# Low attention products of 64 columns between the transposes, and a later head's projection between the two halves

## What is computed

```
xn     = group_norm(x, 32 groups) * w + b
q,k,v  = W_qkv @ xn + b_qkv           # 8 heads of 64 channels
weight = softmax(q^T k * scale)       # 1024 x 1024 for each head
a      = weight @ v
x      = x + W_proj @ a + b_proj
```

## Time and profile before

| | us |
|---|---|
| median of 3 runs | 4347.31 (4347.17 to 4347.99) |
| span of the profiled execution | 4346.0 |
| PE busy in it | 4295.6 |
| DVE / ACT / POOL busy | 3313.6 / 2875.3 / 2505.1 |
| time of the chain that ended last that is PE's | 95% |

### The profile page before, as it was taken

The page is one execution under the profiler, slowest core; times in us unless marked ns, Lnnn a source line. Parts: engine busy times, 40 slices in busy tenths (PEclk is TensorE's granted clock), DMA queues, the critical chain, the costliest instruction groups (busy, mean ns, idle before and its releaser), DMA issues.

```text
span 4346.0 us, 89905 instructions
## 1 busy us (share of the span) xinstructions
PE 4295.6 (99%) x26692; PEld 3736.9 (86%) x26692; DVE 3313.6 (76%) x5483; ACT 2875.3 (66%) x5317; POOL 2505.1 (58%) x2406
## 2 busy tenths in 40 slices
PE   7999999999999999999999999999999999999999
PEld 6888888888888888888888888888888888888887
DVE  5777867788687786777867778687786877868778
ACT  4757747477474775747757476574765747667476
POOL 5655556565564655656566565565655646556465
PEclk9999999999999999999999999999999999999999
DMA  3232222322223222222222222222222222223222
GB/s 87 48 96 47 71 72 48 96 47 80 64 46 96 49 78 64 56 86 49 80 71 66 81 46 80 65 66 79 48 79 64 71 71 49 79 64 82 60 49 92
DMA packets 99933, 295.61 MB, mean 68 GB/s; under 512 B 15136, under 2 KB 15264, under 8 KB 99616
## 3 DMA queue, kind: packets, MB, share of 16 engines
q1 hardware_dynamic: 99616, 291.71, 25.0%
HBM read 123.88 MB, written 33.55 MB: 36 GB/s over the span
## 4 chain that ended last, share of the span: by engine, by line
PE 95%; DVE 2%; issue 1%; POOL 1%; ACT 1%; DMA 0%; SPq 0%; DVEq 0%; ACTq 0%; POOLq 0%
PE ps_t L760 21%; PE ps_g L714 15%; PE ps_o L772 11%; PE ps_o L773 11%; PE ps_s L751 11%; PE ps_s L749 11%; PE ps_s L714 7%; PE ps_t L714 6%; PE ps_o L714 3%; POOL x_raw L389 1%; ACT probs L479 0%; DVE spread L603 0%; DVE pt_lo L569 0%; DVE work L601 0%; PE ps_t L778 0%
## 5 line engine op out<-in xcount | busy, mean ns | idle before, releaser
L383 POOL TENSOR_SCALAR probs<-probs,row_rcp 128x1024 f32<-128x1024 f32 x1024 | 1149.9, 1123 | 1375.5 <-DVE row_rcp L564 1374.0
L560 DVE TENSOR_REDUCE row_min<-ps_s 128x1 f32<-128x1024 f32 x1024 | 1250.2, 1221 | 220.5 <-PE ps_s L751 205.0
L484 ACT CAST pt_hi<-ps_t 128x512 fp32r<-128x512 f32 x2048 | 1110.6, 590 | 446.5 <-PE ps_t L760 431.7
L569 DVE TENSOR_TENSOR pt_lo<-ps_t,pt_hi 128x512 fp32r<-128x512 f32 x2048 | 1308.5, 679 | 9.5 <-ACT pt_hi L484 5.0
L479 ACT ACTIVATE probs<-ps_s,row_min 128x1024 f32<-128x1024 f32 x1024 | 1150.7, 1124 | 215.5 <-DVE row_min L560 202.5
L760 PEld LDWEIGHTS ps_t<-const_sb,probs 128*128 128x128 f32 x8192 | 944.3, 140 | 185.5 <-DVE pt_lo L569 57.0
L760 PE MATMUL ps_t<-const_sb,probs 128*128 128x128 f32 x8192 | 1085.9, 274 | 0.8
L772 PE MATMUL ps_o<-pt_hi,v_st 128*128 128x256 f32 x4096 | 1044.4, 288 | 0.0
L773 PE MATMUL ps_o<-pt_lo,v_st 128*128 128x256 f32 x4096 | 1014.8, 282 | 0.0
L751 PE MATMUL ps_s<-kl_st,q_st 128*128 128x512 f32 x2048 | 808.3, 395 | 0.0
L772 PEld LDWEIGHTS ps_o<-pt_hi,v_st 128*128 128x128 f32 x4096 | 771.6, 188 | 39.4 <-issue 12.4
(11 more groups left out here) (110 smaller groups left out, 4918.2 us busy)
## 6 DMA issues: line engine op xcount, KB each, us to landing
wqk_raw<-in_wqk SPq DMA_DIRECT2D x130, 256.0 KB, 2.7
q_st<-kh_st SPq DMA_DIRECT2D x128, 256.0 KB, 2.9
q_st<-kl_st SPq DMA_DIRECT2D x128, 256.0 KB, 3.6
kh_st<-kh_st SPq DMA_DIRECT2D x128, 256.0 KB, 2.9
kl_st<-kl_st SPq DMA_DIRECT2D x128, 256.0 KB, 3.5
x_raw<-layer_out SPq DMA_DIRECT2D x36, 512.0 KB, 5.0
wv_raw<-in_wv SPq DMA_DIRECT2D x68, 256.0 KB, 3.6
x_raw<-in_x SPq DMA_DIRECT2D x32, 512.0 KB, 5.3
```

Of the source, the lines that this page charges most:

```text
L383: nc.gpsimd.tensor_scalar(probs[m % 2][:, :], probs[m % 2][:, :], row_rcp[:, m % 4:m % 4 + 1], 1.0, ALU.mult, ALU.mult).then_inc(probs_rea ...
L484: nc.scalar.copy(pt_hi[:, m // 2 % 2, 4 * half:4 * half + 4, (m % 2) * P:(m % 2 + 1) * P], ps_t[:, half, :].rearrange("p (b t) -> p b t", ...
L560: nc.vector.tensor_reduce(row_min[:, m % 4:m % 4 + 1], ps_s[:, m % 2, :], AX.X, ALU.min).then_inc(min_ready, 1)
L569: nc.vector.tensor_tensor(pt_lo[place], ps_t[:, half, :].rearrange("p (b t) -> p b t", b=4), f32(pt_hi[place]), ALU.subtract).then_inc(lo_ ...
```

## The change

- `weigh` is split up. The low product of a block (`weigh_low`) takes only the 64 columns of v's high part as the stationary operand and writes partitions 0 to 63 of `ps_o`; the product of v's low part and the probabilities' low part is left out. In odd steps each transpose has one low product behind it. The high products of the group stand in the even step before (seven) and at the end of the odd step (one). Group 7 has its products in the order high, eight low, seven high.
- `later_qk` (and in the last pair the output projection's parts of steps 0 and 1) stands between the transposes of the first and those of the second half, in all steps, where it stood behind both.
- The bias of v moves from `evac_v`, which becomes a copy, to `add_halves`, which becomes one instruction with a scalar operand. `bv_all` and its broadcast transfer of 512 KB give way to `bv_sb`, with 4 KB.

```diff
-            def transpose(n, m):
-                pe.wait_ge(probs_ready, n + 1)
-                for half in range(2):
-                    pe.wait_ge(lo_ready, lo_at(n - 1, half))
-                    for b in range(4):
-                        mm = nc.tensor.transpose(...)
-                    mm.then_inc(transposed, 1)
-            def weigh(tile, g, hd, k, lo, hi):
-                if lo == 0:
-                    pe.wait_ge(attn_ready, sum_at(g - 1))
-                    pe.wait_ge(v_ready, hd + 1)
-                    pe.wait_ge(lo_ready, lo_at(tile + 2 * k + 1, 1))
-                for b in range(lo, hi):
-                    v = v_st[k // 4][:, b, :]
-                    nc.tensor.matmul(ps_o[:, 0:GROUP], v, pt_hi[:, k % 2, b, :], start=(b == 0), stop=False)
-                    mm = nc.tensor.matmul(ps_o[:, 0:GROUP], v, pt_lo[:, k % 2, b, :], start=False, stop=(b == BLK - 1))
+            def transpose(m, c):
+                mm = nc.tensor.transpose(ps_t[:, c // 4, (c % 4) * P:(c % 4 + 1) * P],
+                                         probs[m % 2][:, c * P:(c + 1) * P], ident)
+                if c % 4 == 3:
+                    mm.then_inc(transposed, 1)
+            def weigh_high(k, b):
+                mm = nc.tensor.matmul(ps_o[:, 0:GROUP], v_st[k // 4][:, b, :], pt_hi[:, k % 2, b, :],
+                                      start=(b == 0), stop=(b == BLK - 1))
+                if b == BLK - 1:
+                    mm.then_inc(pv_done, 1)
+            def weigh_low(k, b):
+                nc.tensor.matmul(ps_o[0:D, 0:GROUP], v_st[k // 4][:, b, 0:D], pt_lo[:, k % 2, b, :],
+                                 start=False, stop=False)
+            def group_free(tile, g, hd, k):
+                pe.wait_ge(attn_ready, sum_at(g - 1))
+                pe.wait_ge(v_ready, hd + 1)
+                pe.wait_ge(lo_ready, lo_at(tile + 2 * k + 1, 1))
+            def transpose_and_weigh(n, m, k, between):
+                pe.wait_ge(probs_ready, n + 1)
+                for c in range(BLK):
+                    if c == BLK // 2:
+                        between()
+                    if c % 4 == 0:
+                        pe.wait_ge(lo_ready, lo_at(n - 1, c // 4))
+                    transpose(m, c)
+                    if k is not None and m % 2 == 1:
+                        weigh_low(k, c)
...
+                        transpose_and_weigh(tile + m, m, k, filler)
+                        if k is not None and m % 2 == 0:
+                            group_free(tile, 8 * pair + k, H * i + 2 * p + k // 4, k)
+                            for b in range(BLK - 1):
+                                weigh_high(k, b)
+                        elif k is not None:
+                            weigh_high(k, BLK - 1)
...
-                nc.vector.tensor_tensor(attn[rows, cols], ps_o[rows, 0:GROUP], o_part[k % 2][rows, :],
-                                        ALU.add).then_inc(attn_ready, 1)
+                nc.vector.scalar_tensor_tensor(out=attn[rows, cols], in0=ps_o[rows, 0:GROUP],
+                                               scalar=bv_sb[rows, bass.ds(lay * KT + p, 1)], in1=o_part[k % 2][rows, :],
+                                               op0=ALU.add, op1=ALU.add).then_inc(attn_ready, 1)
...
-                nc.vector.tensor_tensor(v_raw[:, b, :].rearrange("p (o n) -> p o n", o=1),
-                                        v_bank[b].rearrange("p (o n) -> p o n", o=1),
-                                        bv_all[:, bass.ds(lay, 1), :], ALU.add).then_inc(v_evac, 1)
+                nc.vector.tensor_copy(v_raw[:, b, :], v_bank[b]).then_inc(v_evac, 1)
```

More of the change, by code:

```diff
@@ L113, in build @@
         stage = probs + [sb(f"stage{s}", [P, T], F32) for s in range(2)]
-        bv_all = sb("bv_all", [P, LAYERS, C], F32)
         const_sb = sb("const_sb", [P, 2 * P], F32)
@@ L119, in build @@
         bo_sb = sb("bo_sb", [P, LAYERS * KT], F32)
+        bv_sb = sb("bv_sb", [P, LAYERS * KT], F32)
         nw_sb = sb("nw_sb", [P, LAYERS * KT], F32)
@@ L280, in _ @@
             sp.dma_start(nb_sb[:, :], nb).then_inc(const_loaded, 16)
-            sp.dma_start(bv_all[:, :, :], bv.rearrange("(o l) n -> o l n", o=1).broadcast_to([P, LAYERS, C])).then_inc(const_loaded, 16)
+            sp.dma_start(bv_sb[:, :], bv).then_inc(const_loaded, 16)
             load_wqk(0, 0)
@@ L570, in low_part, with add_halves @@
                                         f32(pt_hi[place]), ALU.subtract).then_inc(lo_ready, 1)
-            def add_halves(pair, k):
+            def add_halves(pair, lay, p, k):
                 rows = slice(0, D) if k < 4 else slice(D, P)
@@ L627, in x_low, with evac_v @@
                                         ALU.subtract).then_inc(xn_ready, 1)
-            def evac_v(i, lay, b):
+            def evac_v(i, b):
                 dve.wait_ge(v_acc, 8 * i + b + 1)
-                nc.vector.tensor_tensor(v_raw[:, b, :].rearrange("p (o n) -> p o n", o=1),
-                                        v_bank[b].rearrange("p (o n) -> p o n", o=1),
-                                        bv_all[:, bass.ds(lay, 1), :], ALU.add).then_inc(v_evac, 1)
+                nc.vector.tensor_copy(v_raw[:, b, :], v_bank[b]).then_inc(v_evac, 1)
             def output(i, lay, q):
@@ L662, in _, with pair_steps @@
                 x_low(0, c)
-            def pair_steps(i, p, last):
+            def pair_steps(i, lay, p, last):
                 pair = PAIRS * i + p
@@ L668, in pair_steps @@
                     if not last and m >= 4 and m % 2 == 0:
-                        add_halves(pair, m // 2 - 2)
+                        add_halves(pair, lay, p, m // 2 - 2)
                     if not (last and m + 2 >= PT_STEPS):
@@ L674, in pair_steps @@
                     if m == PT_STEPS - 1 or last and m >= 3 and m % 2 == 1:
-                        add_halves(pair, (m - 3) // 2)
+                        add_halves(pair, lay, p, (m - 3) // 2)
                     if not (last and m + 2 >= PT_STEPS):
@@ L685, in pair_steps @@
                     group_spread(i + 1)
-                add_halves(pair, 7)
+                add_halves(pair, lay, p, 7)
             with dve.Fori(0, PASSES) as i:
@@ L690, in _ @@
                 for b in range(4):
-                    evac_v(i, lay, b)
+                    evac_v(i, b)
                 for m in range(2):
                     smallest(TILES * i + m, m)
-                    evac_v(i, lay, 4 + 2 * m)
+                    evac_v(i, 4 + 2 * m)
                     reciprocal(TILES * i + m, m)
-                    evac_v(i, lay, 5 + 2 * m)
+                    evac_v(i, 5 + 2 * m)
                 with dve.Fori(0, PAIRS - 1) as p:
-                    pair_steps(i, p, False)
-                pair_steps(i, PAIRS - 1, True)
+                    pair_steps(i, lay, p, False)
+                pair_steps(i, lay, PAIRS - 1, True)
                 norm_coefs(i + 1, within(next_pass(i) // B, 0, LAYERS - 1))
@@ new lines, in transpose_and_weigh, with last_group @@
+            def transpose_and_weigh(n, m, k, between):
+                pe.wait_ge(probs_ready, n + 1)
+                for c in range(BLK):
[6 more added lines that the diff above has]
+                        weigh_low(k, c)
+            def last_group(tile, g, hd):
+                group_free(tile, g, hd, 7)
+                weigh_high(7, 0)
+                for b in range(BLK):
+                    weigh_low(7, b)
+                for b in range(1, BLK):
+                    weigh_high(7, b)
@@ L821, in pair_steps, with filler @@
                             project(0, 3, 6)
[L822 to L836, removed]
+                        k = (m - 2) // 2 if m >= 2 else None
+                        def filler():
+                            if not last and m < PT_STEPS - 1:
+                                later_qk(i, m, hd, e, j)
+                            if last and m == 0:
+                                pe.wait_ge(wp_ready, KT * (i // B + 1))
+                                pe.wait_ge(qk_evac, 2 * H * (i + 1))
+                                pe.wait_ge(a_ready, a_at(PAIRS * i + 1, 3))
+                                project(6, 0, 6)
+                            if last and m == 1:
+                                pe.wait_ge(a_ready, a_at(PAIRS * i + 2, 3))
+                                project(6, 6, 9)
+                        transpose_and_weigh(tile + m, m, k, filler)
[5 more added lines that the diff above has]
+                            weigh_high(k, BLK - 1)
                         if not last and m == PT_STEPS - 1:
@@ L872, in _ @@
                     pair = PAIRS * i + p
-                    weigh(TILES * i + PT_STEPS * p, 8 * pair + 7, H * i + 2 * p + 1, 7, 0, BLK)
+                    last_group(TILES * i + PT_STEPS * p, 8 * pair + 7, H * i + 2 * p + 1)
                 pair_steps(i, PAIRS - 1, True)
@@ L880, in _ @@
                     project(q, 0, 9)
```

(4 more changed lines are left out.)

4 lines of the change are left out of this document (removed).

## The result

| | before | after |
|---|---|---|
| median | 4347.65 us | 4684.24 us |
| all runs | 4347.17 to 4349.13 | 4683.79 to 4684.34 |
| ratio, 95% interval | | 1.0773 (1.0758 to 1.0788) |
| span of the profiled execution | 4346.0 us | 4681.8 us |

The change makes the kernel 7.7% slower: 337 us, where 263 were forecast. The direction and the mechanism are those of the prediction; the time lies 34 us above the range.

A forecast was written before the change was run, and what follows sets the result against it. PE, holding 95% of the chain, was taken as the bound; waits of 224 us in 48 pairs and 43 in last pairs, 267 on 4346.0, with small adjustments gave 4610 us, 6% slower, range 4560 to 4650.

The forecast's parts named there:

- The couple of transpose and low product: Odd steps on PE: a transpose with a low product behind it costs 0.228 us, as much as apart; saving zero.
- The first rival: Low product behind a transpose waits for its short load alone, saving 0.05 us per couple: 4450 us; chance 0.20.
- the second: Rival: transposes vanish behind low products, couple 0.119 us, not slower: about 4265 us, or up to 4340; chance 0.11.
- the third: Rival: changing between 128 and 64 columns empties the array, 0.33 us more per couple: about 5600 us; chance 0.03.
- The wait on the evacuation: `later_qk` of steps 4, 8 and 12 waits 1.13 us for the evacuation of `ps_g`, in 48 pairs: 163 us.
- Step 2: Steps 0 and 1 have no products; PE then waits for the low part at step 2, taken as 0.5 us.
- The last pairs: Late `other_half` adds 0.36 us per two steps, six times, and 0.5 at step 2: 2.7 us, 43 in 16 passes.
- the terms of steps 6 and 10: First high product waits for the group's sum, 0.05 us each, between ends of 0 and 0.11.
- of step 14: First high product waits 0.28 us for the group's sum, the projection there having two products, not three.
- of group 7: Group 7 waits 0.40 us for the sum of group 6, made behind the second low part of step 15.
- Bias, copies, first transfer: One DVE instruction replaces another; 0.05 us either way on 512 sums, at most 16 us; taken as zero.
- DVE bound: Addition to the 4610 us sum that, without a worked-out size, gave the range's upper end of 4650 us.

The follow-up runs named there:

- e3: Changed kernel with ACT's evacuation of `ps_g` in steps 3, 7 and 11 moved from behind the exponentials to between the two high parts: 4587.00 us.
- e10: Changed kernel with the projection put back behind both halves of the transposes in steps 0 and 1 alone: 4649.02 us.
- e6: Changed kernel with the bias of v handled as before (plain sum, `bv_all`): 4653.56 us.
- e7: Kernel before with low products 64 columns wide in their old places, the product of the two low parts left out: 4335.88 us.
- e4: Changed kernel with the low products 128 columns wide again, in their new places: 4693.91 us.

## Why the prediction was right in kind and too small

**The couple of transpose and low product** (forecast 0.228, no gain): 0.227 with 64 columns and 0.230 with 128. The reading of the transposes after idle, that a transpose occupies PE for 0.109 and its load for 0.06, held: a load of 64 columns in place of 128 is 53 ns shorter, and the couple changes by 3 ns. The first rival (0.17 to 0.18), the second (0.12) and the third (above 0.3) are refuted by this one number. The profile shows the narrow products as 128*64 among 128*128 transposes, and no emptying of the array between them.

**The wait on the evacuation** (1.13 us, 144 times): 1.1 us, 144 times. Its share of the loss can't be read off one for one: taking it away gave 97 us (e3), not 163, since other waits stood behind it. As the delay that the chain puts on steps 4, 8 and 12, which is what the forecast's sum needs, it was near (3.39 against 3.73 for the three, below).

**Step 2** (0.5 in each pair): 0.55 (e10). **The last pairs** (2.7 us each): 45.88 us in the changed kernel (first transposes at 1118.04 and 1163.92) instead of 43.03, so 2.85.

**The waits for sums** are what failed: the terms of steps 6 and 10 (0.05), of step 14 (0.28) and of group 7 (0.40), and with them the step "Bias, copies, first transfer", which took zero. A pair that isn't last takes 61.37 us (995.30 to 1056.67) instead of 55.38 (926.66 to 982.04): 5.99 more, not 4.67, and 48 x 1.32 is 63 us of the miss of 74. The distances between the steps' first transposes, less PE's own program by the prediction's prices, give its places:

| steps | forecast us | measured us |
|---|---|---|
| 4, 8, 12 | 3 x 1.13 = 3.39 | 1.24 + 1.12 + 1.37 = 3.73 |
| 6, 10 | 2 x 0.05 = 0.10 | 2 x 0.33 = 0.66 |
| 14 | 0.28 | 0.58 |
| 15 and group 7 | 0.40 | 0.55 (0.67 less 0.12 that was there before) |
| 2 (from step 0 on) | 0.50 | 0.48 |

Four sizes were off in the same chain.

- `other_half` comes 1.24 behind the exponentials instead of 1.10; I had read the distance of the evacuation for it.
- The sum with the scalar operand is 0.06 longer, and starts up to 0.25 later.
- Of a wait between 0 and 0.11 I took half, where its upper end was the better reading.
- DVE's low parts come late too, for which there was a term in step 2 alone. The transposes of steps 13 and 15, behind the steps with the shorter projection, wait for them about 0.1 each (the scores before those of step 13 begin at 1041.74 and take 0.93; the transposes begin at 1042.78, not at 1042.67). And at group 7 the sum starts 0.73 behind the second low part (1052.42 to 1053.15), taken as 0.60.

With the first three, step 6 comes out at 0.68 + 0.79 + 1.24 + 0.49 + 0.48 + 0.16 = 3.84 against 3.53, 0.31; measured 0.33. Step 4 is now decided by the sum, not by the evacuation: 0.68 + 0.79 + 1.10 + 0.80 + 0.76 + 0.48 + 0.16 = 4.77 against 3.53, 1.24, as measured. Step 12, with a projection of two products and 0.51 for the sum's start, comes out at 4.52 against 3.30, 1.22, and 0.11 for the low parts: 1.33, measured 1.37. Step 8 alone still goes by the evacuation, with 1.12 for the forecast 1.13.

Of the miss of 74 us the bias is 31 by e6, a little under half; that alone is shown by a run. The rest is an estimate from the rows: 0.14 for `other_half` in steps 6, 10 and 14 makes 20 us in 48 pairs, the halves not taken there 8, the low parts 0.2 a pair or some 10. The last 4 us lie between the forecast and its own sum, since 4346.0 + 267 + 1.3 is 4614 and not 4610. The upper end of the range, 4650, rested on a DVE bound that the prediction doesn't work out, and no run shows one.

## What to carry to other kernels

Before work is moved on an engine that is the bound, follow what the moved work makes late through the engines that only serve it, in their program order, until it comes back as a wait: here a transpose that completed 1.5 us later cost 1.1 us three times a pair, although ACT was busy only two thirds of the time. An engine's order costs nothing until something ahead of the chain is late; then each neighbour on it (a copy that starts only when the instruction before it is over, an operand whose place depends on a loop variable) counts in full. And a distance is to be read from the very instruction that the sum is about: the evacuation's 1.10 stood in for `other_half`'s 1.24, although the trace held both. Two repairs that each work for one order of events need not work together.

## What was not expected of the hardware

- A matmul of 64 stationary columns and 256 moving ones costs 0.0026 us less than one of 128: 10.8 us on 4096 of them (e7), and 10 us in the changed kernel's places (e4).
- A transpose of 128 float32 columns occupies PE for 0.109 us, about what 256 columns of a product do (0.117 to 0.120). With a product behind it the couple takes 0.227, and only 0.003 more when the product's load is 53 ns longer.
- On ACT most neighbours overlap by about 0.1 us, a readout of row sums and the evacuation behind it too. The copies of `other_half` overlap with neither neighbour: they begin 0.02 us behind the end of the one before.
- The sum with a scalar operand whose column is taken from loop variables is 0.06 us longer and, in pairs that aren't last, starts 0.25 and 0.12 us later in two of the eight sums of a pair.
